# Mixture's search, ranks, first lists and first expert placed under the shared expert; the loads of relative attention sorted

## What is computed

```python
def mixture(h, gate, Wg, Wu, Wd, Sg, Su, Sd):
    x = h.reshape(4096, 256)
    scores = softmax(x @ gate.T).T
    weight, index = top_k(scores, 512)
    xg = x[index]
    hidden = gelu(xg @ Wg.T) * (xg @ Wu.T)
    routed = zeros_like(x).at[index].add((hidden @ Wd.T) * weight)
    return routed + (gelu(x @ Sg.T) * (x @ Su.T)) @ Sd.T
```

## Time and profile before

| what | value |
|---|---|
| median of 3 runs | 3858.0 us (3854.7 to 3862.4) |
| the profiled execution, its own time | 3863.8 us |
| its span, first to last instruction | 3861.9 us |
| TensorE (PE) busy | 3522.0 us, 91% |
| VectorE (DVE) busy | 2448.2 us, 63% |
| ScalarE (ACT) busy | 1814.1 us, 47% |
| GpSimd (POOL) busy | 1055.7 us, 27% |
| mean granted TensorE clock | 0.957 of full speed |
| DMA | 390 MB, mean 101 GB/s |

### The profile page before, as it was taken

How to read it: one execution, slowest core, us unless ns; L and a number is a source line. 1 busy time by engine, 2 the same in 40 slices (tenths; PEclk the granted TensorE clock), 3 DMA queues, 4 the chain that set the end, 5 groups by cost and what they waited for, 6 DMA issues and landing times. The chain is left out here.

```text
span 3861.9 us, 92551 instructions
## 1 busy us (share of the span) xinstructions
PE 3522.0 (91%) x33008; PEld 2702.7 (70%) x33008; DVE 2448.2 (63%) x5451; ACT 1814.1 (47%) x3734; POOL 1055.7 (27%) x1031
## 2 busy tenths in 40 slices
PE   5999999999997968999995999999999795999998
PEld 3666666666665857888884777667767684888887
DVE  3676666666665666666753666666666576676664
ACT  1665665665663323444442555445545332444443
POOL 0222222222221002333421433334333101243332
PEclk9999999999998989999996999999999897999999
DMA  4565565565564223434422000000000123343441
GB/s 149 162 172 165 155 176 163 159 177 167 155 176 123 89 93 112 131 102 116 120 65 79 16 21 21 19 19 21 21 19 16 60 87 112 110 120 110 118 117 31
DMA packets 349199, 390.10 MB, mean 101 GB/s; under 512 B 155377, under 2 KB 292721, under 8 KB 335345
## 3 DMA queue, kind: packets, MB, share of 16 engines
q1 hardware_dynamic: 324210, 351.18, 29.3%
q0 software_dynamic: 24576, 33.57, 5.0%
HBM read 246.97 MB, written 137.69 MB: 100 GB/s over the span
## 5 line engine op out<-in xcount | busy, mean ns | idle before, releaser
L2278 POOL TENSOR_TENSOR a_below<-a_probT,a_upper 128x512 f32<-128x512 f32 x128 | 164.2, 1283 | 743.8 <-DVE a_probT L2476 553.4
L2213 ACT ACTIVATE a_prob<-a_ps_s,a_low 128x512 f32<-128x512 f32 x512 | 318.3, 692 | 53.1 <-DVE a_low L2496 52.7
L1377 POOL TENSOR_TENSOR b_prob<-b_prob,b_rinv 128x512 f32<-128x512 f32 (+1 forms) x256 | 237.8, 934 | 383.1 <-DVE b_rinv L1438 383.0
L2060 PE MATMUL a_ps_p<-a_ident,a_prob 128*128 128x128 f32 x2048 | 315.8, 288 | 12.9 <-ACT a_band L2190 9.0
L2496 DVE TENSOR_REDUCE a_low<-a_ps_s 128x2 f32<-128x1024 f32 x256 | 313.5, 1225 | 8.8
L1315 ACT ACTIVATE b_prob<-b_score,b_low 128x256 f32<-128x256 f32 (+1 forms) x512 | 241.8, 474 | 125.4 <-DVE b_low L1433 114.4
L2060 PEld LDWEIGHTS a_ps_p<-a_ident,a_prob 128*128 128x128 f32 x2048 | 222.1, 143 | 101.2 <-issue 75.8
L2186 ACT COPY a_probT<-a_ps_p 128x512 f32<-128x512 f32 x352 | 195.1, 590 | 171.6 <-PE a_ps_p L2060 171.0
L1433 DVE CUSTOM_DVE_ANT_0 b_score<-b_ps_s,b_bias 128x256 f32<-128x256 f32 (+1 forms) x512 | 178.1, 386 | 74.3 <-PE b_ps_s L1256 72.1
L2495 DVE TENSOR_TENSOR a_ps_s<-a_ps_s,a_win 128x320 f32<-128x320 f32 (+1 forms) x256 | 135.0, 527 | 133.5 <-PE a_ps_s L2093 131.0
L611 POOL DMA_INDIRECT out<-ge_eo,ge_index_scatter x64 | 120.7, 1886 | 361.4 <-DVE ge_eo L806 346.7
(11 more groups left out here) (437 smaller groups left out, 10433.6 us busy)
## 6 DMA issues: line engine op xcount, KB each, us to landing
a_win<-band SPq DMA_DIRECT2D x128, 384.0 KB, 5.3
prob<-a_prob SPq DMA_DIRECT2D x128, 384.0 KB, 3.7
shift<-a_gbias SPq DMA_DIRECT2D x64, 256.0 KB, 2.0
a_shifted<-shift SPq DMA_DIRECT2D x256, 64.0 KB, 2.1
a_bins<-prob SPq DMA_DIRECT2D x128, 128.0 KB, 3.7
fe_gT<-in_WgT SPq DMA_DIRECT2D x16, 1024.0 KB
fe_uT<-in_WuT SPq DMA_DIRECT2D x16, 1024.0 KB
fe_dT<-in_WdT SPq DMA_DIRECT2D x16, 1024.0 KB, 4.9
```

The costliest lines, as they stand in the source:

```text
L1377: nc.gpsimd.tensor_tensor(part, part, by_row, ALU.mult).then_inc(divided, 1)
L2060: last = nc.tensor.transpose(bank[:, c * P:(c + 1) * P], prob[:, t % 2, h, 32 + c * P:32 + (c + 1) * P], ident[:, :])
L2213: nc.scalar.activation(prob[:, t % 2, h, 32:32 + T], ps_s[pair][:, r, :], ACT.Exp, bias=low[:, h:h + 1]).then_inc(exped, 1)
L2278: nc.gpsimd.tensor_tensor(below[:, t % 2, :, :], probT[:, t % 2, :, t * P:(t + 1) * P], upper[:, :].unsqueeze(1).to_broadcast([P, HG, P]), ...
```

## The change

**One set of tiles for a mixture.** A class `Mixture` holds the tiles and the semaphores that both stages use, so what the shared stage prepares is found by the expert stage. The shared expert's own weights lie in the places of expert 1's split weights, its x in the tiles of the gathers' rows and of the experts' outputs. Six pieces of 1024 columns make one expert's split weights, as before.

**The shared stage**, now written out for all 32 steps, does this beside its own work:

- search: 30 rounds (the top bit is left out), two in each of steps 0 to 14: one sum between the g half and the u half of the hidden matmuls, one between the halves of the down matmuls;
- step 15 to 20: the three counts, their sums (steps 16, 17, 19), scans, casts; step 21: TensorE turns the parts; step 22: VectorE copies them;
- steps 23 to 30: lists 0, 1 and 2, two steps of VectorE each; finds in steps 25, 27, 29 and slot matmuls in 26, 28, 30, all between the g and the u half;
- expert 0's weights: loaded as soon as the own weights are split, high parts on ScalarE and rests on GpSimd in steps 16 to 21;
- gathers for expert 0 in steps 26 and 27, for expert 1 in 28 and 29;
- expert 0's rows turned and split in steps 30 and 31.

GpSimd does the subtraction for every rest of h and of x (batches 1 to 7), which VectorE did. The own weights are waited for one by one, and TensorE starts without d's. VectorE's finish comes after its second search round and ahead of the ranks' and lists' work of that step. SyncE no longer waits for the last y; GpSimd does so in the expert stage before its first scatter, and VectorE before it overwrites the output tiles.

**The expert stage** starts with expert 0's first step. Lists 3 and on, and everything in the loop, stay. Expert 1's weights are loaded from the stage's start.

**Relative attention**: the 13 loads come in three groups with a semaphore each: ident, table, rows and base (3168 KB); upper, iota, token numbers, scale and three of 256 KB (914 KB); wT and wv (1280 KB). TensorE waits for the first group, and for the last before the projection; VectorE for the first, the second behind its reductions of ident (L2384), the third after the folding; ScalarE for none of them. Up to base, 4592 KB were in the queue behind x, now 3168 KB.

```diff
+def sum_pe(nc, pe, k, table, count, ps_c, counted, summed):
+    pe.wait_ge(counted, k + 1)
+    nc.tensor.matmul(ps_c, table[:, :], count[:, :], start=True, stop=True).then_inc(summed, 1)
...
+def load_weights(sp, mix, e, m, dram):
+    sp.dma_start(mix.whole[m][:, :, :].rearrange("p k i -> p (k i)"), dram[ds(e, 1)].rearrange("a p k i -> p (a k i)")).then_inc(mix.w_in[m], 16)
...
+def rest_weights(ops, engine, mix, e, q, m):
+    w, high, rest = mix.piece(q, m)
+    engine.wait_ge(mix.w_high, PIECES * e + m + 1)
+    ops.tensor_tensor(rest, w, high.bitcast(F32), ALU.subtract).then_inc(mix.w_split, 1)
...
+LISTS = 3
+RANK = SEARCH // 2
+PARTS_AT = RANK + 6
+LISTS_AT = RANK + 8
+WEIGHTS_AT = RANK + 1
+ROWS_AT = HB_S * B - KC
...
+            sp.dma_start(gT, own[0]).then_inc(own_in[0], 16)
+            sp.dma_start(uT, own[1]).then_inc(own_in[1], 16)
+            load_xT(0, 0)
+            sp.dma_start(dT, own[2]).then_inc(own_in[2], 16)
...
+            for m in range(3):
+                sp.wait_ge(own_split, (KC, 2 * KC, PIECES)[m])
+                load_weights(sp, mix, 0, m, experts[m])
...
+                    sp.wait_ge(t_split, KC * n + KC)
                     load_xT(n + 2, p)
...
+            def places(step):
+                r, at = (step - LISTS_AT) // 2, (step - LISTS_AT) % 2
+                if step < RANK:
+                    sum_pe(nc, pe, 2 * step, same, count, ps_c, counted, summed)
+                if step == RANK + 1:
+                    sum_pe(nc, pe, SEARCH, same, count, ps_c, counted, summed)
...
+                if step == PARTS_AT:
+                    pe.wait_ge(parts_ready, 1)
...
+                if 1 <= r <= LISTS and at == 0:
+                    if r == 1:
+                        pe.wait_ge(parts_taken, 2)
+                    for quarter in range(QUARTERS):
+                        find_pe(nc, pe, mix, r - 1, quarter)
+                if 1 <= r <= LISTS and at == 1:
+                    place_slots_pe(nc, pe, mix, r - 1)
+            for step in range(STEPS):
...
+                pe.wait_ge(h_ready, step + 1)
+                half_hidden_pe(nc, xb, g, j, ps_g[j % 2])
+                places(step)
+                half_hidden_pe(nc, xb, u, j, ps_u[j % 2]).then_inc(gu_ready, 1)
+                if step == LAG:
+                    pe.wait_ge(own_split, PIECES)
+                if step >= LAG:
+                    down(step - LAG, range(0, NT // 2))
+                if step < RANK:
+                    sum_pe(nc, pe, 2 * step + 1, same, count, ps_c, counted, summed)
+                if step >= LAG:
+                    down(step - LAG, range(NT // 2, NT)).then_inc(down_done, 1)
+                if step >= ROWS_AT:
+                    transpose_rows_pe(nc, pe, mix, 0, 0, 0, step - ROWS_AT)
...
+        @block.gpsimd
+        def _(pool):
+            for step in range(STEPS):
+                n, j = step // HB, step % HB
+                pool.wait_ge(hh_ready, step + 1)
+                nc.gpsimd.tensor_tensor(h[1][:, j, :], raw[:, j % 2, :], h[0][:, j, :].bitcast(F32), ALU.subtract).then_inc(hs_ready, 1)
+                if j == 0 and n + 1 < B:
+                    pool.wait_ge(t_high, KC * (n + 1) + KC)
+                    for k in range(KC):
+                        nc.gpsimd.tensor_tensor(xs[1][:, 1 - n % 2, k, :], xT[1 - n % 2][:, k, :], xs[0][:, 1 - n % 2, k, :].bitcast(F32),
+                                                ALU.subtract).then_inc(t_split, 1)
+                if WEIGHTS_AT <= step < WEIGHTS_AT + PIECES:
+                    rest_weights(nc.gpsimd, pool, mix, 0, 0, step - WEIGHTS_AT)
+                first = step - LISTS_AT - 3
+                if 0 <= first < 4:
+                    r = first // 2
+                    if first % 2 == 0:
+                        hold(pool, mix.list_ready, r + 1, mix.held)
+                        take_index_pool(nc, pool, mix, 0, r, r)
+                    for t in range(2 * (first % 2), 2 * (first % 2) + 2):
+                        gather_pool(nc, pool, mix, rows_xn, r, t)
...
+            def places(step):
+                if step == RANK:
+                    total(st[:, :], ALU.is_gt, thr[:, :])
...
+                if step == RANK + 3:
+                    ch.link(nc.vector.scalar_tensor_tensor(equal, pos, need[:, :], equal, ALU.is_le, ALU.mult))
+                    ch.link(nc.vector.scalar_tensor_tensor(sel, st[:, :], thr[:, :], equal, ALU.is_gt, ALU.add))
+                    total(sel, ALU.mult, 1.0)
...
+                if step >= LISTS_AT and at == 0:
+                    if 1 <= r <= LISTS:
+                        take_dve(nc, dve, mix, r - 1)
+                    if r < LISTS:
+                        hits_dve(nc, mix, ch, r)
+                        hot_dve(nc, mix, r, 0)
+                if step >= LISTS_AT and at == 1:
+                    if 1 <= r <= LISTS:
+                        lists_dve(nc, dve, mix, ch, r - 1)
+                    if r < LISTS:
+                        for quarter in range(1, QUARTERS):
+                            hot_dve(nc, mix, r, quarter)
...
+            for step in range(STEPS):
+                n, j = step // HB, step % HB
+                if step < RANK:
+                    search_dve(nc, dve, ch, 2 * step, search, summed, counted)
+                product_dve(nc, dve, step, j, ps_u, gelu, raw, gelu_ready, hs_ready, h_ready)
+                if step < RANK:
+                    search_dve(nc, dve, ch, 2 * step + 1, search, summed, counted)
+                if j == LAG - 1 and n > 0:
+                    finish(n - 1)
+                places(step)
+                if step >= ROWS_AT:
+                    rest_rows_dve(nc, dve, mix, 0, 0, step - ROWS_AT)
+            finish(B - 1)
...
-            for r in range(3):
-                pe.wait_ge(counted, r + 1)
-                table = same if r == 0 else before
-                nc.tensor.matmul(ps_c, table, count[:, :], start=True, stop=True).then_inc(summed, 1)
...
-            for r in range(AHEAD - 1):
-                for quarter in range(QUARTERS):
-                    find(r, quarter)
-                place_slots(r)
-            for k in range(KC):
-                transpose_rows(0, 0, 0, k)
-            pe.wait_ge(parts_taken, 2)
...
+                if early:
+                    dve.wait_ge(y_out[q], mix.STORED)
+                else:
                     dve.wait_ge(added[q], START_ROWS + DONE * i)
...
-            def whole_list(r):
-                hits(r, ch)
...
-            whole_list(0)
-            for m in range(0, UP // 2):
-                split_w(0, 0, m)
-            take(0)
-            lists(0, ch)
-            whole_list(1)
-            for m in range(UP // 2, UP):
-                split_w(0, 0, m)
-            take(1)
-            lists(1, ch)
-            for k in range(KC):
-                split_x(0, 0, k)
-            for m in range(UP, EACH):
-                split_w(0, 0, m)
-            whole_list(2)
-            take(2)
-            lists(2, ch)
...
+        first_loads = ((ident, const["ident"]), (whole_table, table_d), (rows, rows_d), (whole_base, base_d))
+        small_loads = ((upper, const["upper"]), (iota, const["iota"]), (number, const["token"]), (scale, const["row_scale"]),
+                       (bins_w, bins_d), (bins_b, bins_base_d), (vbase, vbase_d))
+        w_loads = ((wT, wT_d[0]), (wv, wT_d[1]))
...
+            for loads, sem in ((first_loads, const_in), (small_loads, small_in), (w_loads, w_in)):
+                for tile, dram in loads:
+                    sp.dma_start(tile[tuple(slice(None) for _ in tile.shape)], dram).then_inc(sem, 16)
...
-            pe.wait_ge(const_in, 16 * len(loads))
...
+            pe.wait_ge(w_in, 16 * len(w_loads))
...
-            act.wait_ge(const_in, 16 * len(loads))
...
+            dve.wait_ge(const_in, 16 * len(first_loads))
```

754 lines of the change are left out of this document (353 added, 401 removed).

## The result

| | us |
|---|---|
| before, median of 4 runs beside the changed kernel | 3859.8 (3854.7 to 3862.4) |
| changed kernel, median of 4 runs | 3797.0 (3791.8 to 3800.2) |
| ratio | 0.9845, 95% interval 0.9828 to 0.9863 |
| profiled execution of the changed kernel | 3796.6, span 3794.8 |

The gain is 62.8 us; 94.1 were forecast, and 3797.0 lies 1 us above the range. The sum was made against the profiled execution, and there 3769.7 stands against 3796.6: 26.9 us too little. The changed kernel was run again later, beside other runs of before: 3789.4 against 3851.5, again 62.1 us apart.

A forecast was written before the change was run, and what follows sets the result against it. TensorE was taken to bound the shared expert, except for a 49.5 us hole behind it. Terms 1 to 5 gave 43.9 us a mixture, twice 87.8, plus 6.3: 94.1 off the profiled 3863.8; 3764 against the median, range 3751 to 3796.

The forecast's parts named there:

- Term 1: Between shared expert and expert 0: TensorE's hole of 49.5 us closes to 3.0, gain 46.5 us a mixture.
- Terms 2 and 3: Shared expert starts earlier, gain 3.1 us; expert 0's first three steps get shorter, gain 4.3 us; each a mixture.
- Term 3: Expert 0's first three steps: 15.1 us become 10.8, including some 2 us for a start at lower clock.
- Term 6: Shared expert: GpSimd's rests and gathers, ScalarE's weight pieces and the loads are covered and cost nothing.
- rival A: Steps 15 to 31: GpSimd and VectorE hold each other up, 10 us a mixture, 3784 us; chance 0.14.
- term 5: Shared expert: TensorE's new waits on VectorE's search, ranks and lists, loss 4.2 us a mixture (0 to 8.4).
- Rival C: Shared expert: pauses in 15 search steps drop TensorE to 1.2 GHz, 132 us lost, 3896 us; chance 0.04.
- Term 4: Shared expert: finds, transposes and slot matmuls moved into TensorE's queue, loss 5.8 us a mixture.
- Rival B: Shared expert: search loop sets the pace, each of 32 steps 1 us late, 3828 us; chance 0.10.
- Term 7: Relative attention's start, once: sorted loads let base land at 13.3 and VectorE start at 16.3, gain 6.3 us.

The follow-up runs named there:

- x3: Changed kernel with all rests (h, x, weights) on VectorE from step 15 on, GpSimd then doing only gathers: 3771.3 us, ratio 0.9786.
- x4: Changed kernel with every rest on VectorE in all 32 steps, GpSimd doing only gathers in the shared stage: 3771.7 us, ratio 0.9793.
- x5: As x3, but the six weights' rests stand in steps 15, 16, 22, 26, 29 and 30: 3769.5 us, ratio 0.9780.
- x8: x5 with TensorE's third sum (step 19) and turning of the parts (step 21) moved between the down matmuls' halves: 3759.9 us, ratio 0.9751.
- x2: Changed kernel with expert 0's weights split in steps 6 to 11 instead of 16 to 21, still on GpSimd: 3788.1 us, ratio 0.9826.
- x7: Kernel before with only relative attention's three groups of loads and their waits from the change: 3848.8 us, ratio 0.9992.

## Why the prediction was wrong, step by step

The difference of the two spans is 67.1 us. By the timelines it splits like this (loss negative):

| | forecast | first mixture | second |
|---|---|---|---|
| 1 hole | 46.5 | 46.5 | 46.5 |
| 2 start of the shared expert | 3.1 | 2.7 | 3.2 |
| 3 expert 0's first steps | 4.3 | 5.1 | 5.5 |
| 4, 5 matmuls and waits in the shared expert | -10.0 | -24.1 | -27.3 |
| 7 relative attention, at its end | 6.3 | 4.7 | |
| unchanged stages | 0 | 0.7 | 3.7 (window attention between) |

The 4.4 us of the unchanged stages were in nobody's forecast and are not explained; that the miss isn't larger by them is luck.

**Term 1** was right to a tenth: finish, store's issue and boundary fill 3.0 us, and no landing of y, no weight and no row was missing. **Terms 2 and 3** were within 1.2 us of their size. Term 3's reason "a hole of 3 us will not keep it" holds for some executions only: behind the same hole of 3.0 us the granted clock falls in the changed kernel (three steps in 10.0 and 9.7 us) and stays at 1.00 in x3's first and x4's second mixture (9.0 and 8.5 us). The issue of expert 1's weights at the stage's start had no cost that shows.

**Term 6** is the step that failed: "GpSimd's rests" were "costed at nothing, with its cover". The working asked only whether GpSimd would be in time, and it was: TensorE waited 0.2 us for a rest of h. What it takes from VectorE while it works was left to rival A. With it, 14.8 and 16.0 us of waits stand where term 5 had 4.2. By the table, the changed kernel's 170.7 and 173.9 are 10.6 and 13.8 above x3, where only the engine of the rests from step 15 on differs, and 12.4 and 15.6 above x5. Without those rests on GpSimd term 5 was nearly right: in x5, with the ranks in the same places, the waits are 3.1 + 1.5 + 0.6 + 0.6 + 0.2 = 6.0 us, or 3.9 more than the 2.1 of the kernel before, and the stage is 11.8 us longer than before, where terms 4 and 5 said 10.0.

In the ranks something comes on top. TensorE, idle for 4.8 us in step 19, resumes at the lower clock (0.71 and 0.61 in the windows above). Step 19 lasts 12.1 us; in x8, without a wait, 4.4. Of the difference of 7.7 the wait is 4.8 and the slower matmuls are 2.9. Rival C thus came for one step instead of fifteen (in the second mixture for two, 19 and 21, which lasts 12.4 us there).

**Rival A** is what happened, with 0.14. Its mechanism and place were right; its 10 us a mixture were 0.6 to 3.8 short against x3, 2.4 to 5.6 against x5. The 2.4 us weights' rests fell on the ranks' chain, where each microsecond is TensorE's (x2 takes them out and the ranks fall by 6 to 8 us), and the clock fell there. The argument against it failed: "its 128x512 operation, beside a busy VectorE, averages 1.28, with no sign of a hold". The hold falls on whoever comes second, so it has to be looked for on VectorE as well; and in relative attention VectorE's operations of 128x512 and more have an operand in PSUM, all but 14 (the kernel before, 100 to 1240 us):

```profile
L161 DVE TENSOR_TENSOR a_x_rest<-a_xT,a_x_high 128x512 fp32r<-128x512 f32 x14 | 9.0, 683 | 0.0
```

**Term 4** was right, with term 5, to two microseconds in x5; of that run's 11.8 us, 3.9 are waits, and 7.9 are left for term 4's 5.8. Part of this is a slip in the sum: it takes 0.3 for three pairs of slot matmuls that it puts at 0.3 each, so its own prices give 6.4. The pieces that term 5 names likewise add up to 4.8 us (5.5 with the one-hots of all three lists), not to 4.2, unless the waits that go are set against them. Rival B, each search step 1 us late, did not come: the second round costs a step 0.28 us of matmul (4.64 against 4.36), as the sum that later steps no longer have gives back 0.23 each (4.13).

**Term 7** was right where it was worked out: base landed at 12.58 (13.3 forecast), VectorE started at 16.23 (16.3), the first projection at 34.62 (34.8 forecast, 41.14 before). That 6.5 us at the start are 6.3 at the end of the stage was assumed. The trace shows 4.7, x7's 10.7 (1247.2 to 1236.5); the runs of x7 show a gain of 2.7 us, with an interval from a loss of 3 to a gain of 9. Neither 0 nor 6.3 is excluded: the time that TensorE spends at 1.2 GHz behind the start varies by more.

## What to carry to other kernels

Work moved to an idle GpSimd is not free for VectorE: list VectorE's operations that read two SBUF tiles or only convert, and put GpSimd's elsewhere in time, or do on VectorE in 0.7 us what holds it for 1.3. Where two engines may hold each other up, a row speaks against it only if operations of the kinds that can meet do meet in it. When the total varies by more than the part that is changed, measure that part by the starts of its steps. And read TensorE's clock from the spacing of equal matmuls as well as from the granted clock: ahead of its first entry that record said 1.00 here for 40 us of matmuls at half speed.

## What the runs showed of the hardware that was not expected

- GpSimd's 128x512 subtraction (1.28 us) delayed a VectorE operation of one column: the search's bitwise or, 0.16 us in all 29 cases in x4, took 1.17 to 1.21 in four of 29 beside the rests. So a very short operation can wait for almost the whole of the subtraction.
- GpSimd needs 1.29 us for a 128x512 rest and 2.4 for 128x1024, VectorE 0.69 and 1.22; so moving a rest can cost VectorE, in waiting, more than it saves.
- The same code ran at 1.2 GHz from 34 us until 38.0, 42, 63 or 74.5 us, and relative attention ended 1227.6 to 1242.5 us from the start. The granted clock of the profile says 1.00 up to these times.
